# A shorter way from the filters' network to the first unit of a long convolution

## Chip, cores and metric

One core of one Trainium2 chip. The time is the device time of one launch, in microseconds. A measurement is the median of several runs.

## What is computed

The input `x` has 4 images of 64 channels, 256 by 256. Two layers follow each other.

Layer one is a long convolution. Two small networks (X and Y) turn a position embedding `z` (256 x 33) into 64 filters of length 256 each:

```
h = sin(freq * (z @ w1 + b1))
h = sin(freq * (h @ w2 + b2))
h = sin(freq * (h @ w3 + b3))
hx or hy = (h @ wo) * exp(-t * |deltas|)
k[c] = outer(hx[:, c], hy[:, c])
y = x (*) k, causal in both directions, + x * bias[c]
```

Since the kernel of each channel is an outer product, the convolution is one product with a triangular Toeplitz matrix along the rows and one along the columns.

Layer two whitens the channels: the covariance of every ninth sample (64 x 64), its inverse square root by five Newton-Schulz steps, and `out = deconv @ (y - mean)`.

## The kernel before

Everything runs in one program, with an order written out by hand for each engine and semaphores between them. The work has three parts.

**The head.** SP loads `first` (w1 of both networks and z transposed, L202), `columns` (biases and frequency, L203), `hidden` (w2, w3, wo, L208, after POOL has zeroed their place, L337), four x tiles (L216) and the bias (L262). PE makes the first product (L620) once all four parameter loads are in (`params_loaded`, L619). For each of three layers DVE adds the bias and multiplies by the frequency (L465), reduces the argument to the range of the sine table with two steps that find the whole number of turns (L467, L468), three that subtract it times a three-part 2 pi (L470), and a clamp (L471). ACT takes the sine (L417) and PE makes the next product (L624). Between the first layer's argument and the second's, DVE also computes the sampling mask (L474 to L478). At the end DVE scales the decay (L482) and multiplies (L485): `filt` holds 128 filters of 384 values (`filt_ready`).

**The way to the first unit.** SP stores `filt` to DRAM (L265), waits until it has landed, and loads the Hankel tiles of units 0, 1 and 2 (L232, two DMAs per unit, 128 rows of 256 values, each row one value further on, all from this one copy). Then it stores 15 more copies (L271), waits for all of them (`copies_stored`, L273), and only then loads the tiles of units 3 and 4, and in its main loop those of later units, from the 16 copies. For each unit ACT reverses the tile (L391 in fp32, L392 rounded), and DVE makes the remainder of the rounding (L499). For x, ACT rounds (L401) and POOL makes the remainder (L334).

**The units.** There are 128 units (2 sweeps x 64 channels). A unit is V(q) = 16 products in `make_v` and Y(q) = 16 products in `make_y`, both through `toeplitz` (L633 to L636: high by high, high by low, low by high, and one small fp32 product for the other block). PE's order is V(0), V(1), Y(0), V(2), Y(1), V(3), Y(2) and so on. ACT and DVE take V from PSUM (L408, L410, L490), DVE finishes Y (L510), POOL masks it for the covariance (L368) and DVE sums it (L518). SP stores Y to DRAM. Units 0 to 63 and 64 to 127 each cover two images. After them come the covariance (L665), the Newton-Schulz steps (L709 to L728) and the last stage: 64 tiles are read back, multiplied (L744), shifted (L442, L613) and stored to `out` (L287).

SP's queue holds its DMAs in the order written: a wait in it holds back every later DMA. ACT, DVE, POOL and PE go through their lists in order too.

Of the kernel before, what the change touches and what calls it, by code (L numbers as in the profile page):

```python
# [6 lines left out]
F32 = mybir.dt.float32  # L7
# [6 lines left out]
P = 128  # L14
# [15 lines left out]
PI_HI = 6.28125  # L30
PI_MID = math.floor((TWO_PI - PI_HI) * 2.0 ** 21) / 2.0 ** 21
PI_LO = TWO_PI - PI_HI - PI_MID
# [30 lines left out]
def conv_whiten(nc, x, first, hidden, columns, bias, out):  # L63
    g_dram = nc.dram_tensor("filters", [COPIES, COPY_PITCH], F32, kind="Internal").ap()
    y_dram = nc.dram_tensor("convolved", [SWEEPS * P, ROWS * XW], F32, kind="Internal").ap()

    with ExitStack() as ctx:
# [44 lines left out]
        col = sb("col", [P, 4])  # L112
# [3 lines left out]
        arg, turns, hid, pos_f, pos, decay = (kept[:, k * S:(k + 1) * S] for k in range(6))  # L116
# [25 lines left out]
        params_loaded, bias_loaded, w_zeroed = sem("params_loaded"), sem("bias_loaded"), sem("w_zeroed")  # L142
# [5 lines left out]
        copies_stored = sem("copies_stored")  # L148
        x_loaded = [sem(f"x_loaded{k}") for k in range(X_SLOTS)]
# [51 lines left out]
        def _(sp):  # L201
            sp.dma_start(first_sb, first).then_inc(params_loaded, 16)  # L202
            sp.dma_start(col[:], columns).then_inc(params_loaded, 16)  # L203

            sp.wait_ge(w_zeroed, 1)
            for k in range(2):
                h = slice(k * ORDER, (k + 1) * ORDER)
                sp.dma_start(w_sb[h, :, h], hidden[h, :].rearrange("p (l n) -> p l n", l=3)  # L208
                             ).then_inc(params_loaded, 16)
# [8 lines left out]
            def load_hankel(q):  # L218
# [6 lines left out]
                for f in range(2):  # L225
                    at = (f * C + q % C) * GLEN
                    if q < H_SLOTS:
                        src = bass.AP(tensor=g_dram.tensor, offset=at, ap=[[1, P], [1, S]])
                    else:
                        src = bass.AP(tensor=g_dram.tensor, offset=at,  # L230
                                      ap=[[COPY_PITCH + P // COPIES, COPIES], [1, P // COPIES], [1, S]])
# [87 lines left out]
        def _(pool):  # L319
# [16 lines left out]

            nc.gpsimd.memset(w_sb, 0.0).then_inc(w_zeroed, 1)  # L337
# [45 lines left out]
        def _(act):  # L383
            def flip(q):
# [3 lines left out]
                act.wait_ge(hankel_loaded[h], 32 * (q // H_SLOTS + 1))  # L388
# [57 lines left out]
        def _(dve):  # L446
# [14 lines left out]
            dve.wait_ge(params_loaded, 16 * 4)  # L461
            for layer in range(3):

                dve.wait_ge(f_mm, layer + 1)
                chained(nc.vector.tensor_scalar(arg, ps[:, 0, 0:S], col[:, layer:layer + 1], col[:, 3:4],  # L465
                                                ALU.add, ALU.mult))
                chained(nc.vector.tensor_scalar(turns, arg, 1.0 / TWO_PI, MAGIC, ALU.mult, ALU.add))  # L467
                chained(nc.vector.tensor_scalar(turns, turns, MAGIC, None, ALU.subtract))  # L468
                for part in (PI_HI, PI_MID, PI_LO):
                    chained(nc.vector.scalar_tensor_tensor(arg, turns, -part, arg, ALU.mult, ALU.add))  # L470
                nc.vector.tensor_scalar(arg, arg, PI_BELOW, -PI_BELOW, ALU.min, ALU.max).then_inc(f_dve, 1)  # L471
                if layer == 0:
                    dve.wait_ge(index_ready, 1)
                    chained(nc.vector.tensor_copy(idx, index.bitcast(I32)))  # L474
# [303 lines left out]
```

## Time and profile before

| | us |
|---|---|
| median of 3 runs | 952.86 |
| lowest and highest of them | 945.55, 954.18 |
| the profiled execution, its own time | 948.63 |
| its span in the profile | 946.5 |
| V(0) begins on PE | 29.67 |
| last product of the last unit | 641 |

The time of the profiled execution is 2.1 us more than its span; these lie around what the profile records. Products in fp32 are recorded as two instructions each. The profile gives the granted TensorE clock as a share of 2.4 GHz. Its record of the clock here begins at about 34.5 us; ahead of that the column says 1.00 in every slice, also where products take twice as long as later, so that in the head the level has to be read from the length of the products.

### The profile page before, as it was taken

To read this page: it belongs to the slowest core of one execution; us is meant where nothing else is said; L and a number is where in the kernel's file an instruction comes from. 1 tells how busy PE (TensorE), PEld (TensorE's weight loads), DVE (VectorE), ACT (ScalarE), POOL (GpSimd) and SP (SyncE) were. 2 spreads that over 40 slices of the span, in tenths; PEclk is the share of its full clock that TensorE was granted. 3 is DMA by queue.
4 is the path that set the end of the run, shared out by engine and by line. 5 is a ranking of instruction groups with operands and counts; after the bars stand their busy time and mean duration, and the time that the engine had idled before them with its cause. 6 is when DMAs were issued, how large, how long until landed. Compare 5 with 4: busy or idle time off the path is not lost.

```text
span 946.5 us, 15709 instructions
## 1 busy us (share of the span) xinstructions
PE 868.5 (92%) x5970; PEld 729.9 (77%) x5970; DVE 576.3 (61%) x641; ACT 401.0 (42%) x715; POOL 494.5 (52%) x278
## 2 busy tenths in 40 slices
PE   2799999999999999999999999999999997777774
PEld 0799999999999999999999999999544442322221
DVE  5388787788888847878777878784333332222222
ACT  2355555555555525555555555550233322222221
POOL 2298888888888856878777778771000000000000
PEclk9999999999999999999999999999999999999998
DMA  2799998999999866999999999988499999999998
GB/s 105 218 315 293 284 283 276 297 278 291 279 287 287 283 218 194 341 335 339 329 343 332 357 334 330 340 279 331 170 413 422 421 423 427 427 427 427 427 428 360
DMA packets 99351, 306.36 MB, mean 324 GB/s; under 512 B 13484, under 2 KB 48333, under 8 KB 84685
## 3 DMA queue, kind: packets, MB, share of 16 engines
q1 hardware_dynamic: 99276, 305.37, 90.8%
q8 instruction: 47, 0.77, 0.3%
q14 instruction: 28, 0.22, 0.1%
HBM read 167.96 MB, written 137.36 MB: 323 GB/s over the span
## 4 chain that ended last, share of the span: by engine, by line
PE 77%; DMA 18%; DVE 3%; issue 1%; ACT 0%; SPq 0%; DVEq 0%; ACTq 0%
PE ps L636 24%; DMA out<-z_all 17%; PE ps L633 13%; PE ps L634 13%; PE ps L635 13%; PE ps L744 10%; PE ps L665 3%; DVE z_all L613 1%; DVE kept L470 1%; PE ps L684 0%; DMA plain<-filters 0%; PE ps L624 0%; ACT z_all L442 0%; DMA kept<-hidden 0%; PE ps L721 0%
## 5 line engine op out<-in xcount | busy, mean ns | idle before, releaser
L633 PE MATMUL ps<-rounded 128*128 128x256 f32 x1024 | 373.7, 365 | 10.3 <-DVE rounded L499 8.7
L368 POOL TENSOR_TENSOR masked_all<-y_all,mask 128x1024 f32<-128x1024 f32 x126 | 326.3, 2590 | 63.3 <-DVE y_all L510 63.1
L635 PE MATMUL ps<-rounded 128*128 128x256 f32 x1024 | 289.5, 283 | 0.0
L634 PE MATMUL ps<-rounded 128*128 128x256 f32 x1024 | 288.4, 282 | 0.0
L510 DVE SCALAR_TENSOR_TENSOR y_all<-x_all,bias_sb,ps 128x1024 f32<-128x1024 f32 x127 | 162.5, 1280 | 96.8 <-DMA convolved<-y_all 60.5
L334 POOL TENSOR_TENSOR rounded<-x_all,rounded 128x512 fp32r<-128x512 f32 x128 | 165.1, 1290 | 83.1 <-ACT rounded L401 82.5
L633 PEld LDWEIGHTS ps<-rounded 128*128 128x128 f32 x1024 | 196.5, 192 | 11.8 <-issue 11.4
L636 PE MATMUL ps<-plain,x_all 128*128 128x128 f32 x1024 | 197.4, 274 | 0.0
L634 PEld LDWEIGHTS ps<-rounded 128*128 128x128 f32 x1024 | 197.3, 193 | 0.0
L636 PE MATMUL ps<-plain 128*128 128x128 f32 x1024 | 196.4, 273 | 0.0
L635 PEld LDWEIGHTS ps<-rounded 128*128 128x128 f32 x1024 | 192.9, 188 | 0.0
L744 PE MATMUL ps<-kept,z_all 128*128 128x512 f32 x344 | 152.3, 596 | 22.2 <-ACT z_all L442 17.2
L636 PEld LDWEIGHTS ps<-plain,x_all 128*128 128x128 f32 x1024 | 159.0, 191 | 0.0
L636 PEld LDWEIGHTS ps<-plain 128*128 128x128 f32 x1024 | 158.0, 190 | 0.0
L518 DVE TENSOR_REDUCE z_all<-masked_all 128x116 f32<-128x1044 f32 x126 | 155.5, 1234 | 0.0
L744 PEld LDWEIGHTS ps<-kept,z_all 128*128 128x128 f32 x344 | 63.8, 190 | 109.7 <-issue 109.7
L613 DVE TENSOR_SCALAR z_all<-ps,small 128x1024 f32<-128x1024 f32 x48 | 61.6, 1284 | 140.6 <-PE ps L744 75.4
L408 ACT COPY plain<-ps 128x512 f32<-128x512 f32 x128 | 75.0, 586 | 156.1 <-PE ps L636 155.7
L442 ACT ACTIVATE z_all<-ps,small 128x1024 f32<-128x1024 f32 x48 | 53.4, 1113 | 157.2 <-DMA out<-z_all 102.9
L401 ACT CAST rounded<-x_all 128x512 fp32r<-128x512 f32 x128 | 80.2, 626 | 77.4 <-DMA x_all<-x 77.0
L490 DVE TENSOR_TENSOR rounded<-ps,rounded 128x512 fp32r<-128x512 f32 x128 | 87.9, 686 | 28.1 <-ACT rounded L410 27.9
L499 DVE TENSOR_TENSOR rounded<-plain,rounded 128x512 fp32r<-128x512 f32 x128 | 90.7, 709 | 13.4 <-ACT rounded L392 13.4
(103 smaller groups left out, 479.8 us busy)
## 6 DMA issues: line engine op xcount, KB each, us to landing
x_all<-x SPq DMA_DIRECT2D x128, 512.0 KB, 5.6
convolved<-y_all SPq DMA_DIRECT2D x256, 256.0 KB, 5.3
out<-z_all SPq DMA_DIRECT2D x48, 1024.0 KB, 15.7
plain<-filters SPq DMA_DIRECT2D x256, 128.0 KB, 4.8
kept<-convolved SPq DMA_DIRECT2D x29, 1024.0 KB, 19.9
out<-masked_all SPq DMA_DIRECT2D x16, 1024.0 KB, 15.2
kept<-convolved SPq DMA_DIRECT2D x28, 512.0 KB, 6.3
rounded<-convolved SPq DMA_DIRECT2D x9, 1024.0 KB, 20.2
```

The lines of the kernel that those rows point to most:

```text
L334: nc.gpsimd.tensor_tensor(x_lo[k], row_block(q % X_SLOTS, 0), x_hi[k].bitcast(F32), ALU.subtract).then_inc(x_lo_done, 1)
L368: nc.gpsimd.tensor_tensor(masked_of(k, 0, PER), by_image(y_sb[k]), mask_of(q // C, 0, PER), ALU.mult).then_inc(masked_done, 1)
L401: nc.scalar.copy(x_hi[q % 2], row_block(k, 0)).then_inc(x_hi_done, 1)
L490: nc.vector.tensor_tensor(v_lo[k], ps_v[k][:, :, 0:S], v_hi[k].bitcast(F32), ALU.subtract).then_inc(v_lo_done, 1)
L499: nc.vector.tensor_tensor(t_lo[k], hankel[h][:, :, ::-1], t_hi[k].bitcast(F32), ALU.subtract).then_inc(t_lo_done, 1)
L510: nc.vector.scalar_tensor_tensor(y_sb[k], x_sb[q % X_SLOTS], bias_sb[:, q % C:q % C + 1], ps_y[k].rearrange("p a n -> p (a n)"), ALU.mult, ...
L518: nc.vector.tensor_reduce(z_of(q % C), grouped(q % 2, 0, BLOCKS), AX_X, ALU.add).then_inc(z_done, 1)
L633: mm(wide, hi[:, b, cols], t_hi[k][:, f, :], start=True, stop=False)
L634: mm(wide, hi[:, b, cols], t_lo[k][:, f, :], start=False, stop=False)
L635: mm(wide, lo[:, b, cols], t_hi[k][:, f, :], start=False, stop=False)
L636: last = mm(o[:, b, m * S + P:(m + 1) * S], block1[:, b, cols], t_f32[k][:, f, :], start=False, stop=True)
L744: last = mm(ps[:, bank(t, u) + r, :], dmat, t_in[k][:, w:w + IMG], start=True, stop=True)
```

## The change

Three groups of edits:

- **Sine arguments in turns.** A fifth column of `col` gets the frequency divided by 2 pi (once, after `columns` has landed). Per layer DVE now makes three steps: bias and frequency (out of PSUM), adding a constant that rounds to a whole number, and `(rounded - constant) - arg`. The sine takes this remainder with a scale of -2 x 3.1415925. The scaling of the decay moves ahead of the layers, the mask behind `filt_ready`. ACT's `round_x(0)` and `round_x(1)` move behind the sines of the first and the second layer.
- **Own stores and loads for unit 0.** The two filters of unit 0 are stored first, each in one DMA that writes 16 copies of 384 values to a tensor of their own, and loaded from there. The general store is issued between these stores and loads. Every other load stays as it is, in the same order. ACT, DVE and PE take unit 0 filter by filter: V(0) waits for the first filter alone, Y(0) for the second.
- **Products on zeros in pauses.** PE makes 128 x 128 fp32 products on a zeroed tile (POOL zeroes it first of all): 4 ahead of the first product, 4, 6 and 6 in the pauses of the three layers, 22 after the last. The first product waits for `first` alone, the second for `hidden`.

The diff, cut to its core:

```diff
+        rest = kept[:, 14 * S + MASK_COLS:15 * S + MASK_COLS]
+        idle = y_all[:, 0:P]
...
@@ SP @@
                 for f in range(2):
                     at = (f * C + q % C) * GLEN
+                    spread = [[COPY_PITCH + P // COPIES, COPIES], [1, P // COPIES], [1, S]]
+                    if q == 0:
+                        sp.wait_ge(first_stored, 16 * 2)
+                        src = bass.AP(tensor=first_dram.tensor, offset=f * GLEN, ap=spread)
+                        sp.dma_start(hankel[k][:, f, :], src).then_inc(first_hankel[f], 16)
+                        continue
...
             sp.wait_ge(filt_ready, 1)
+            for f in range(2):
+                sp.dma_start(bass.AP(tensor=first_dram.tensor, offset=f * GLEN,
+                                     ap=[[0, 1], [COPY_PITCH, COPIES], [1, GLEN]]),
+                             filt[f * C:f * C + 1, :].unsqueeze(1).to_broadcast([1, COPIES, GLEN])
+                             ).then_inc(first_stored, 16)
             sp.dma_start(bass.AP(tensor=g_dram.tensor, offset=0, ap=[[GLEN, 2 * C], [1, GLEN]]), filt
                          ).then_inc(filt_stored, 16)
+            load_hankel(0)
             sp.wait_ge(filt_stored, 16)
-            for q in range(H_SLOTS):
+            for q in range(1, H_SLOTS):
                 load_hankel(q)
@@ POOL @@
+            nc.gpsimd.memset(idle, 0.0).then_inc(idle_ready, 1)
             nc.gpsimd.memset(w_sb, 0.0).then_inc(w_zeroed, 1)
@@ ACT @@
-            round_x(0)
             for layer in range(3):
                 act.wait_ge(f_dve, layer + 1)
-                nc.scalar.activation(hid, arg, ACT.Sin).then_inc(f_sin, 1)
-            round_x(1)
-            flip(0)
+                nc.scalar.activation(hid, rest, ACT.Sin, scale=-2.0 * PI_BELOW).then_inc(f_sin, 1)
+                if layer < 2:
+                    round_x(layer)
+            for f in range(2):
+                act.wait_ge(first_hankel[f], 16)
+                nc.scalar.copy(t_hi[0][:, f, :], hankel[0][:, f, ::-1]).then_inc(first_hi, 1)
+                flat = nc.scalar.copy(t_f32[0][:, f, :], hankel[0][:, f, :P - 1:-1])
+                flat.then_inc(flipped if f else first_flat, 1)
@@ DVE @@
-            dve.wait_ge(params_loaded, 16 * 4)
+            dve.wait_ge(columns_loaded, 16)
+            nc.vector.tensor_scalar(col[:, 4:5], col[:, 3:4], 1.0 / TWO_PI, None, ALU.mult).then_inc(turns_ready, 1)
+            dve.wait_ge(decay_ready, 1)
+            nc.vector.tensor_scalar(decay[0:C, :], decay[0:C, :], 1.0 / (2 * S), None, ALU.mult).then_inc(turns_ready, 1)
+            dve.wait_ge(turns_ready, 2)
             for layer in range(3):
                 dve.wait_ge(f_mm, layer + 1)
-                chained(nc.vector.tensor_scalar(arg, ps[:, 0, 0:S], col[:, layer:layer + 1], col[:, 3:4],
+                chained(nc.vector.tensor_scalar(arg, ps[:, 0, 0:S], col[:, layer:layer + 1], col[:, 4:5],
                                                 ALU.add, ALU.mult))
-                chained(nc.vector.tensor_scalar(turns, arg, 1.0 / TWO_PI, MAGIC, ALU.mult, ALU.add))
-                chained(nc.vector.tensor_scalar(turns, turns, MAGIC, None, ALU.subtract))
-                for part in (PI_HI, PI_MID, PI_LO):
-                    chained(nc.vector.scalar_tensor_tensor(arg, turns, -part, arg, ALU.mult, ALU.add))
-                nc.vector.tensor_scalar(arg, arg, PI_BELOW, -PI_BELOW, ALU.min, ALU.max).then_inc(f_dve, 1)
+                chained(nc.vector.tensor_scalar(near_int, arg, MAGIC, None, ALU.add))
+                nc.vector.scalar_tensor_tensor(rest, near_int, MAGIC, arg, ALU.subtract, ALU.subtract
+                                               ).then_inc(f_dve, 1)
...
-            split_t(0)
+            for f in range(2):
+                dve.wait_ge(first_hi, f + 1)
+                split = nc.vector.tensor_tensor(t_lo[0][:, f, :], hankel[0][:, f, ::-1],
+                                                t_hi[0][:, f, :].bitcast(F32), ALU.subtract)
+                split.then_inc(t_lo_done if f else first_lo, 1)
@@ PE @@
+            def warm_up(n):
+                for _ in range(n):
+                    mm(ps[:, 5, 0:P], idle, idle, start=True, stop=True)
+            pe.wait_ge(idle_ready, 1)
+            warm_up(4)
+            pe.wait_ge(first_loaded, 16)
             mm(ps[:, 0, 0:S], first_sb[:, 0:2 * ORDER], first_sb[:, 2 * ORDER:], start=True, stop=True
                ).then_inc(f_mm, 1)
             for layer in range(3):
+                warm_up(4 if layer == 0 else 6)
+                if layer == 0:
+                    pe.wait_ge(hidden_loaded, 16 * 2)
                 pe.wait_ge(f_sin, layer + 1)
                 mm(ps[:, 0, 0:S], w_sb[:, layer, :], hid, start=True, stop=True).then_inc(f_mm, 1)
+            warm_up(22)
             pe.wait_ge(filt_ready, 1)
```

## Rows read from the trace of the kernel before

**Rows 1.** The page: span and busy time of each engine.
```profile
span 946.5 us, 15709 instructions
...
PE 868.5 (92%) x5970; PEld 729.9 (77%) x5970; DVE 576.3 (61%) x641; ACT 401.0 (42%) x715; POOL 494.5 (52%) x278
```

**Rows 2.** Stages: length, busy (instructions) of PE, PEld, DVE, ACT, POOL, clock, DMA share, GB/s.
```profile
29.60:34.50 4.90, 4.83 (x22) 4.86 (x23) 0.69 (x1) 0.63 (x2) 0.00 (x0) 1.00 1.04 375
34.50:60.00 25.50, 24.54 (x210) 24.27 (x210) 16.73 (x19) 14.72 (x30) 16.97 (x9) 1.00 0.82 256
...
100.00:460.00 360.00, 359.55 (x3110) 359.39 (x3109) 276.26 (x300) 188.38 (x375) 291.31 (x151) 1.00 0.90 287
```

**Rows 3.** Timeline of the sine layers: start, length, engine, line, operation, idle before.
```profile
0.73 0.43 SPq L202 DMA_DIRECT2D kept<-first  x1
...
4.63 1.22 PE L620 MATMUL ps<-kept 33*128 33x256 f32 x2 [4.63 <-DMA kept<-hidden]
...
5.97 0.54 DVE L465 TENSOR_SCALAR kept<-ps,col 128x256 f32<-128x256 f32 x1 [3.20 <-PE ps L620]
...
7.20 2.29 DVE L470 SCALAR_TENSOR_TENSOR kept<-kept 128x256 f32<-128x256 f32 x3
...
7.76 1.45 POOL L334 TENSOR_TENSOR rounded<-x_all,rounded 128x512 fp32r<-128x512 f32 x1 [4.84 <-ACT rounded L401]
...
16.39 0.54 DVE L465 TENSOR_SCALAR kept<-ps,col 128x256 f32<-128x256 f32 x1 [1.83 <-PE ps L624]
16.97 0.29 DVE L467 TENSOR_SCALAR kept<-kept 128x256 f32<-128x256 f32 x1
...
17.62 1.34 DVE L470 SCALAR_TENSOR_TENSOR kept<-kept 128x256 f32<-128x256 f32 x3
...
19.33 0.42 ACT L417 ACTIVATE kept<-kept 128x256 f32<-128x256 f32 x1 [4.32 <-DVE kept L471]
...
21.16 0.42 DVE L485 TENSOR_TENSOR kept<-ps,kept 128x256 f32<-128x256 f32 x1 [1.09 <-PE ps L624]
```

**Rows 4.** The chain of waits: the second load of the hidden weights.
```profile
2.36 2.23 DMA kept<-hidden
```

**Rows 5.** Timeline of SP's queue: the DMA issues from the filters' store on.
```profile
21.61 0.33 SPq L265 DMA_DIRECT2D filters<-kept  x1
23.48 2.69 SPq L232 DMA_DIRECT2D plain<-filters  x6
26.21 8.44 SPq L271 DMA_DIRECT2D filters<-kept  x15
38.91 3.39 SPq L232 DMA_DIRECT2D plain<-filters  x4
```

**Rows 6.** Timeline, from the first filters loaded to the first unit.
```profile
27.87 0.40 ACT L391 COPY plain<-plain 128x256 f32<-128x256 f32 x1 [7.62 <-DMA plain<-filters]
...
29.67 0.55 PE L633 MATMUL ps<-rounded 128*128 128x256 f32 x1 [8.65 <-DVE rounded L499]
```

**Rows 7.** Timeline of PE at the fourth unit.
```profile
44.66 0.36 PE L633 MATMUL ps<-rounded 128*128 128x256 f32 x1 [0.96 <-issue]
```

**Rows 8.** Timeline of PE in the small matrix products.
```profile
657.30 0.83 PE L684 MATMUL ps<-ident 128*128 128x128 f32 x6
...
661.12 0.49 PE L713 MATMUL ps<-z_all 128*128 128x128 f32 x2
```

**Rows 9.** Table of stages: the loads from one copy, then the copies.
```profile
24.50:26.50 2.00, 0.00 (x0) 0.00 (x0) 0.00 (x0) 0.00 (x0) 0.00 (x0) 1.00 0.62 95
31.00:35.00 4.00, 4.00 (x22) 4.00 (x21) 0.00 (x0) 0.69 (x2) 0.00 (x0) 1.00 1.07 397
```

**Rows 10.** Table of stages: the last stage, and its end.
```profile
669.00:946.00 277.00, 227.88 (x515) 94.77 (x514) 82.33 (x65) 71.25 (x64) 0.00 (x0) 0.99 0.97 405
936.00:938.00 2.00, 0.34 (x1) 0.00 (x0) 1.28 (x1) 1.11 (x1) 0.00 (x0) 1.00 1.00 422
939.00:940.00 1.00, 0.00 (x0) 0.00 (x0) 0.00 (x0) 0.00 (x0) 0.00 (x0) 0.56 1.03 434
```

More of the change, by code:

```diff
@@ L111, in conv_whiten @@
         small = sb("small", [P, 8])
-        col = sb("col", [P, 4])
+        col = sb("col", [P, 5])
         chan_i, chan, rate = sb("chan_i", [P, 1], I32), sb("chan", [P, 1]), sb("rate", [P, 1])
-        arg, turns, hid, pos_f, pos, decay = (kept[:, k * S:(k + 1) * S] for k in range(6))
+        arg, near_int, hid, pos_f, pos, decay = (kept[:, k * S:(k + 1) * S] for k in range(6))
+        rest = kept[:, 14 * S + MASK_COLS:15 * S + MASK_COLS]
+        idle = y_all[:, 0:P]
         pos_i = pos_f.bitcast(I32)
@@ L140, in conv_whiten @@
         ps_y = [ps[:, 4 + 2 * k:6 + 2 * k, :] for k in range(2)]
-        params_loaded, bias_loaded, w_zeroed = sem("params_loaded"), sem("bias_loaded"), sem("w_zeroed")
+        first_loaded, columns_loaded, hidden_loaded = sem("first_loaded"), sem("columns_loaded"), sem("hidden_loaded")
+        bias_loaded, w_zeroed, idle_ready = sem("bias_loaded"), sem("w_zeroed"), sem("idle_ready")
+        first_stored, first_hankel = sem("first_stored"), [sem(f"first_hankel{f}") for f in range(2)]
+        first_hi, first_flat, first_lo = sem("first_hi"), sem("first_flat"), sem("first_lo")
         pool_step, ident_ready = sem("pool_step"), sem("ident_ready")
@@ L201, in _ @@
         def _(sp):
-            sp.dma_start(first_sb, first).then_inc(params_loaded, 16)
-            sp.dma_start(col[:], columns).then_inc(params_loaded, 16)
+            sp.dma_start(first_sb, first).then_inc(first_loaded, 16)
+            sp.dma_start(col[:, 0:4], columns).then_inc(columns_loaded, 16)
             sp.wait_ge(w_zeroed, 1)
@@ L229, in load_hankel @@
                     else:
-                        src = bass.AP(tensor=g_dram.tensor, offset=at,
-                                      ap=[[COPY_PITCH + P // COPIES, COPIES], [1, P // COPIES], [1, S]])
+                        src = bass.AP(tensor=g_dram.tensor, offset=at, ap=spread)
                     sp.dma_start(hankel[k][:, f, :], src).then_inc(hankel_loaded[k], 16)
@@ L387, in flip @@
                 k, h = q % T_SLOTS, q % H_SLOTS
-                act.wait_ge(hankel_loaded[h], 32 * (q // H_SLOTS + 1))
+                act.wait_ge(hankel_loaded[h], 32 * (q // H_SLOTS + (1 if h else 0)))
                 wait(act, y_mm, q - T_SLOTS + 1)
@@ L485, in _ @@
             nc.vector.tensor_tensor(filt[:, 0:S], ps[:, 0, 0:S], decay, ALU.mult).then_inc(filt_ready, 1)
+            dve.wait_ge(index_ready, 1)
+            chained(nc.vector.tensor_copy(idx, index.bitcast(I32)))
+            chained(nc.vector.tensor_scalar(near, idx, 1.0 / STRIDE, MAGIC, ALU.mult, ALU.add))
+            chained(nc.vector.tensor_scalar(near, near, MAGIC, float(STRIDE), ALU.subtract, ALU.mult))
+            chained(nc.vector.tensor_tensor(idx, idx, near, ALU.subtract))
+            nc.vector.tensor_scalar(mask[:], idx, 0.0, None, ALU.is_equal).then_inc(mask_ready, 1)
             def split_v(q):
@@ L644, in make_v @@
                 pe.wait_ge(x_lo_done, q + 1)
-                pe.wait_ge(t_lo_done, q + 1)
+                if q == 0:
+                    pe.wait_ge(first_flat, 1)
+                    pe.wait_ge(first_lo, 1)
+                else:
+                    pe.wait_ge(t_lo_done, q + 1)
                 wait(pe, v_lo_done, q - 1)
@@ L654, in make_y @@
                 pe.wait_ge(v_lo_done, q + 1)
+                if q == 0:
+                    pe.wait_ge(flipped, 1)
+                    pe.wait_ge(t_lo_done, 1)
                 wait(pe, y_done, q - 1)
```

17 lines of the change are left out of this document (3 added, 14 removed).

## The prediction, made before the changed kernel ran

> **What bounds the kernel now.** I read the page first, then the table of stages, then the timeline of the first 45 us engine by engine, SP's queue last. PE is busy for 868.5 of 946.5 us [rows 1], and from 100 to 460 us for 359.55 of 360 [rows 2]. So in the units PE is the bound and has no slack, and whatever lets it begin them sooner comes off the end, if nothing stops it again. The last stage (L744) follows them in order, so it shifts too.
>
> The head is one chain, of which the reader should see the single links [rows 3]. The first product starts at 4.63, when the second load of `hidden` has landed (2.23 after its issue, [rows 4]), and DVE takes it at 5.97. A quiet layer (the third) costs DVE 16.39 to 19.29: 0.58 for L465, 0.33 each for L467 and L468, 1.38 for the three L470, 0.30 for the clamp, starts to starts. In the first layer L470 took 2.29 instead of 1.34, because its last one ran into POOL's split of x (L334, 7.76 to 9.21). `filt` is ready at 21.16 + 0.42 = 21.58. Call this F.
>
> From F on, SP's queue sets the pace [rows 5]: the store at F + 0.03, six loads from F + 1.90, fifteen copies from F + 4.63 to F + 13.1, and, once all have landed, the loads of units 3 and 4 from F + 17.33. The first tile is there at 27.87, V(0) starts at 29.67 = F + 8.1 [rows 6]. V(0) and what follows run at half rate at first: 22 records in 4.9 us against 210 in 25.5 [rows 2]. The record of the clock begins only at 34.5, so the length of the products says that this was the lower level, 1.2 GHz.
>
> One short line is what matters most here: V(3) starts at 44.66 = F + 23.1, after 0.96 us of idle PE [rows 7]. It needs unit 3's tile, whose load SP issues only after all 15 copies have landed, and it follows that issue by 44.66 - 38.91 = 5.75 us. So the units are already caught once by a chain that hangs on F and not on when V(0) began.
>
> **The change, part by part: F.**
> - First product. It waits for `first` alone, issued at 0.73 [rows 3]; with 2.23 to landing [rows 4] that is 2.96. Four products on zeros ahead of it, at the low level 2 x 0.22 each (at the upper level six records, three products, took 0.83 with their tail, [rows 8]), are 1.8 us; if POOL's zeroing ends by 1.1 (an estimate) they end by 2.9. I take 3.0 (2.7 to 3.5). DVE takes the result 1.34 later, at 4.35; its new tiny step and the moved scaling of the decay hang on the exponential, which I put at 3.5, and end near 4.0: hidden, by 0.3.
> - Layer one: L465 0.58, one step like L467 0.33, one like a single L470 0.44, then 0.04 to the sine, 0.42 of sine (L417), 0.05 to PE: done at 6.2. The table load lies ahead of this, behind the exponential. `hidden` was in at 4.63. The second product starts at 6.2 and is taken at 7.55 at the low level.
> - Layer two: its last step would start at 8.45. It has two SBUF inputs, as L470 has, and round_x(0) still ends at about 7.7, since x lands when it did, so POOL's split runs at 7.76 to 9.21 as before. The step then ends at about 9.5 as its like did in [rows 3], 0.6 late. Sine and product follow at 10.0.
> - Layer three: I take PE at the upper level by now (it has been busy nearly without a break since 1.1; before, it rose after 4.9 us of work, [rows 2]). A product of 128 columns takes 0.49 [rows 8], 256 columns 0.21 more, so 0.70 for 1.22. DVE begins at 10.8, its last step at 11.7. POOL's second split (L334) now follows round_x(1), which ends near 10.6, and runs to about 12.0; the step ends at 12.25, 0.1 to 0.5 late. Sine, product 12.75 to 13.5, L485 0.42: F = 14.05.
>
> F thus moves from 21.58 to 14.05, 7.5 us. Without both collisions and with the upper level from the second product on it is 12.6 (9.0 us); with the low level throughout and 6 products on zeros of 0.44 sticking out of a pause of about 2.0 it is 15.0 (6.6 us). The mask (5 steps, 9.8 to 11.6 in the old timeline) hides behind SP's transfers now. The zero products cost nothing in the pauses: 6 x 0.22 = 1.3 against 2.0.
>
> The GPSIMD Engine Reference of the Trainium skill (section Specifications) says that this engine's SBUF interface is shared with VectorE and contends with DVE instructions that have two SBUF inputs. The 2.29 above agrees. By it the two collisions stand; without it F would be some 0.7 to 1.2 earlier.
>
> **From F to V(1).** Two small stores and the general one are issued in about 1.0 (0.33 each, L265), the small ones have landed by F + 2.3 (the store before took 1.87 from issue to the loads), then unit 0's loads take 0.6 to 0.85 each of SP (4 from the copies took 3.39, [rows 5]), so units 1 and 2 are loaded from F + 3.7 instead of F + 2.8. A load with one filter less behind it to reverse and split puts V(0) at F + 6.1 to F + 6.6, against 8.1. If the 22 products on zeros (4.8 us at the upper level, up to 7.3 if it rises on the way) kept the clock, V(0) takes 2.3 instead of 4.3. But V(1) needs unit 1's whole tile: 3.7 + 4.4 (first load to first tile, 23.48 to 27.87) + 1.8 (tile to PE, [rows 6]) = F + 9.8. PE then idles about 1.3. V(1), Y(0), V(2), Y(1) are 64 products, 9.3 us at the upper level, so PE is done at F + 19.1.
>
> **From F to V(3).** Nothing in this part of the chain was shortened. Copies are issued from F + 5.4 instead of F + 4.6. Against that, four loads come from the one copy for six. These run at 95 GB/s where the copies reach 397 [rows 9], so they drag on everything behind them. The two fewer would give 2.4 us if nothing else counted, the later issue takes 0.8. I bound the net at -0.8 to +1.6 and take +0.5: the end of the copies is set by the 397 GB/s, and most of the drag was ahead of it. V(3) is at F + 22.6 = 36.65, against 44.66: 8.0 earlier. PE idles 3.5 us before it, where it was 0.96.
>
> **The clock after this wait.** At 0.96 of idle the upper level held. At the end of the kernel the granted clock is 0.56 in 939 to 940 [rows 10], so it fell at about 939.1, 2.8 us after the last product (0.34 busy after 936). 3.5 us of idle is nearer to this than to 0.96, so I take it that PE falls to the lower level ahead of V(3) and pays again what the head paid: 4.9 us at half rate, 2.4 us. Bounds: 0 and 3.4.
>
> The page TensorE: Matmul & The Clock Gate of the Trainium skill (section on HAM oscillation) tells of a kernel in which DMA waits between short bursts of products brought each burst back to the lower level. By it the fall comes; the last rows of this trace speak for it.
>
> **Sum.** 7.5 (F) + 0.5 (copies) - 2.4 (clock) = 5.6 us. The profiled execution goes from 948.63 to 943.0. The median of the runs shown is 952.86, 4.2 above it, and I forecast for the median: 947.3. The lead at V(0), 29.67 to 20.4, is 9.3 us, and most of what the own stores and loads and the warm clock give over F's gain is thrown away at V(3).
>
> **Rivals.**
> 1. The copies' wait doesn't bind (they land by F + 13). Then what counts is V(1): 33.93 (V(0) of 16 products at 1.07 per four from 29.67) against 14.05 + 9.8 = 23.85, plus 0.3 of slow V(1) and the old 0.96: 11.3 us, 941.5. For it: fewer hot loads. Against it: issue alone needs 8.4 us from F + 5.4, which makes 13.8 even with no landing.
> 2. The clock holds at V(3). 8.0 us, 944.9. For it: 3.5 is a guess by half a microsecond each way, and slow early units would shorten the idle. Against: the 2.8 above.
> 3. Slower than before: the new DRAM tensor lies between `filters` and `convolved` and shifts the latter, which the last stage reads while it writes `out`, 277 us from 669 on at a DMA share near 1 [rows 10]. If the new place lowers this rate by 2% it costs 5.6 us and the gain is gone; from there on it is slower: 4% gives 958. For it: runs of one kernel lie 8.6 us apart, so something in DMA or placement moves it by 0.9%. Against: sizes and strides of `convolved` stay.
> 4. The change does not do what it says: products on zeros don't raise the clock, or they queue in front of the real ones. F = 15.0, PE late everywhere, V(3) after a shorter idle: 6.6 + 0.5 = 7.1 if the clock then holds, 4.7 if not; 946 to 948. It can't be told from the forecast by time, only in the profile.
>
> **How the numbers follow.** Forecast 0.50, rival 1 0.13, rival 2 0.24, rival 3 0.07, rival 4 0.06. A change within 1% (9.5 us) is about what a measurement of this kernel can't tell from none. Forecast, rival 2 and rival 4 lie inside it, rival 1 beyond. Since F alone is open by 1.5 and the measurement by some 3 us, I give a tenth of the forecast and a quarter of rival 2 to faster by over 1%: 0.13 + 0.05 + 0.06 = 0.24. Slower by over 1% needs a rate 5.5% down in rival 3: 0.03. The range runs from 938.5 (rival 1 and a good measurement) to 953.0 (forecast with low F, and the mild half of rival 3).
>
> **What would show it.** Right: F near 14.0, with a DVE step of 0.8 to 1.1 for 0.44 in layers two and three beside POOL's L334; products of 0.70 from the third on; V(0) near 20.4, V(1) near 23.9; a wait of 3 to 4 us before V(3) near 36.6, and 22 records in the next 4 to 5 us. Wrong: V(3) without such a wait (rival 1), products at full rate behind it (rival 2), a last stage longer than 277 us (rival 3), slow products at F (rival 4). The forecast fails outright if F is above 16, or the copies land before F + 14.

## The result, and the profile after

| | us |
|---|---|
| changed kernel, median of 20 runs | 946.17 (942.85 to 952.54) |
| kernel before, median of 20 runs beside them | 952.53 |
| ratio | 0.9948, interval 0.993 to 0.9965 |
| profiled execution, its own time and span | 945.89, 944.1 |

The ratio is taken over the fast executions alone (one of the kernel before, at 1009.42 us, is left out) and is not the quotient of the two medians, which is 0.9933, or 6.4 us. By the ratio the change gains 0.52%, about 5.0 us; 5.6 were forecast, and a median of 947.3. It was measured twice more beside the experiments: 0.9931 (0.9905 to 0.9957) and 0.9947 (0.9918 to 0.9975). The total came out, but not each of its terms: the part from F to V(3) was forecast 2.2 us too short.

The page of the changed kernel: span and busy time.

```profile
span 944.1 us, 15874 instructions
...
PE 880.8 (93%) x6054; PEld 742.9 (79%) x6054; DVE 573.5 (61%) x631; ACT 402.0 (43%) x717; POOL 494.1 (52%) x279
```

PE has 84 records more, the 42 products on zeros. Its busy time therefore grows while the kernel gets shorter; a busy share says nothing about the end here.

The layers in the timeline of the changed kernel (start, length, engine, line and operation, in brackets idle before and what ended it; they answer to [rows 3]):

```profile
3.00 1.22 PE L654 MATMUL ps<-kept 33*128 33x256 f32 x2
...
7.68 1.27 POOL L350 TENSOR_TENSOR rounded<-x_all,rounded 128x512 fp32r<-128x512 f32 x1 [4.61 <-ACT rounded L419]
8.14 1.19 DVE L495 TENSOR_SCALAR kept<-kept 128x256 f32<-128x256 f32 x1
...
9.37 0.55 DVE L496 SCALAR_TENSOR_TENSOR kept<-kept 128x256 f32<-128x256 f32 x1
...
11.90 0.55 DVE L495 TENSOR_SCALAR kept<-kept 128x256 f32<-128x256 f32 x1
...
13.41 0.70 PE L661 MATMUL ps<-kept 128*128 128x256 f32 x2 [0.86 <-ACT kept L434]
...
14.25 0.42 DVE L501 TENSOR_TENSOR kept<-ps,kept 128x256 f32<-128x256 f32 x1 [1.34 <-PE ps L661]
```

The first product starts at 3.00 (forecast 3.0). The collision in layer two is there, but one step earlier than forecast: beside POOL's split of x (L350, 7.68) it is L495, with a single SBUF input, that takes 1.19 us for 0.29. The next step starts only at 9.37. In layer three the same line takes 0.55 beside the second split. The last product takes 0.70 as forecast. F is 14.25 + 0.42 = 14.67, against 21.58 before and 14.05 forecast: 6.9 us for 7.5.

SP's queue from F on (it answers to [rows 5]):

```profile
14.70 1.19 SPq L276 DMA_DIRECT2D first_filters<-kept  x2
15.94 0.58 SPq L280 DMA_DIRECT2D filters<-kept  x1
17.98 1.21 SPq L235 DMA_DIRECT2D plain<-first_filters  x2
19.23 2.01 SPq L241 DMA_DIRECT2D plain<-filters  x4
21.28 8.97 SPq L287 DMA_DIRECT2D filters<-kept  x15
34.47 2.45 SPq L241 DMA_DIRECT2D plain<-filters  x4
```

The two small stores take 0.6 each to issue, where one general store took 0.33; the general store behind them now takes 0.58, so it is not their shape alone. They have landed 3.3 after F, not 2.3. Unit 1's load is issued at F + 4.6 for a forecast 3.7, the copies at F + 6.6 for 5.4. The last copy has landed at 34.47, F + 19.8. Before it was F + 17.3.

PE's waits (they answer to [rows 6, 7]):

```profile
21.43 0.36 PE L672 MATMUL ps<-rounded 128*128 128x256 f32 x1 [2.41 <-DVE rounded L545]
...
26.00 0.36 PE L672 MATMUL ps<-rounded 128*128 128x256 f32 x1 [2.02 <-DVE rounded L522]
...
39.50 0.55 PE L672 MATMUL ps<-rounded 128*128 128x256 f32 x1 [4.05 <-issue]
```

V(0) leads the old one by 8.24 us (29.67 to 21.43), V(1) waits 2.0, and V(3) waits 4.05 and leads by 5.16 only (44.66 to 39.50). Then the clock (stages: length, busy time of PE, PEld, DVE, ACT, POOL, granted clock, DMA share, GB/s):

```profile
25.00:31.00 6.00, 5.00 (x43) 5.04 (x44) 3.25 (x5) 4.03 (x9) 2.04 (x2) 1.00 1.04 381
32.00:34.50 2.50, 2.50 (x24) 2.50 (x24) 0.16 (x1) 0.00 (x0) 2.26 (x1) 1.00 0.11 41
37.00:38.00 1.00, 0.00 (x0) 0.00 (x0) 0.00 (x0) 0.25 (x1) 0.00 (x0) 0.97 0.68 200
38.00:44.00 6.00, 4.50 (x21) 4.53 (x22) 3.12 (x4) 3.09 (x7) 1.33 (x2) 0.50 0.93 269
44.50:45.00 0.50, 0.50 (x5) 0.50 (x4) 0.50 (x1) 0.50 (x2) 0.50 (x1) 0.72 0.96 361
```

The copies fill the DMA to 31 or so (381 GB/s). From 32 to 34.5 nearly nothing moves, yet the last landing comes at 34.47. The granted clock falls to the lower level just ahead of 38 (0.97 in that slice, 0.50 to 44) and comes back at 44.8. PE had been idle since 35.46, so it fell 2.5 us into the idle stretch, and the products from 39.5 to 44.8 ran at half rate: 5.3 us, of which 2.6 are lost (forecast 4.9 and 2.4).

The start of the first covariance (the products of 129 columns behind the first sweep's units) is a mark that lies ahead of the second sweep. Before, and after:

```profile
341.85 3.40 PE L665 MATMUL ps<-z_all 128*128 128x129 f32 x29
```
```profile
338.94 6.31 PE L711 MATMUL ps<-z_all 128*128 128x129 f32 x55
```

2.91 us of lead are left: 5.16 at V(3) less the 2.64 of clock is 2.5 and accounts for all but 0.4 of them. The two profiled spans differ by 2.4 us. The medians differ by more: the old kernel's profiled execution (948.63) lay 3.9 us under its median, and the new one (945.89) 0.3 under its own.

### The profile page after: what moved, and what is told of

The parts are those of the page before. It is cut to its first block, busy times and chain, and to the rows that moved or that the text cites. A ratio compares the mean times of both kernels' runs of the same rounds, so it can differ in the third digit from the quotient of the medians.

```text
span 944.1 us, 15874 instructions
## 1 busy us (share of the span) xinstructions
PE 880.8 (93%) x6054; PEld 742.9 (79%) x6054; DVE 573.5 (61%) x631; ACT 402.0 (43%) x717; POOL 494.1 (52%) x279
## 4 chain that ended last, share of the span: by engine, by line
PE 66%; DMA 24%; DVE 4%; SPq 3%; issue 1%; ACT 0%; DVEq 0%; POOL 0%; ACTq 0%; POOLq 0%
PE ps L675 20%; DMA out<-z_all 17%; PE ps L672 11%; PE ps L673 11%; PE ps L674 11%; PE ps L790 10%; DMA convolved<-y_all 6%; PE ps L711 3%; DVE y_all L533 1%; DVE z_all L640 1%; SPq L251 1%; SPq L241 1%; SPq L220 1%; DMA plain<-filters 0%; PE ps L730 0%
## 5 line engine op out<-in xcount | busy, mean ns | idle before, releaser
L350 POOL TENSOR_TENSOR rounded<-x_all,rounded 128x512 fp32r<-128x512 f32 x128 | 164.9, 1288 | 73.7 <-ACT rounded L419 72.5
```

The lines of the kernel that those rows point to most:

```text
L350: nc.gpsimd.tensor_tensor(x_lo[k], row_block(q % X_SLOTS, 0), x_hi[k].bitcast(F32), ALU.subtract).then_inc(x_lo_done, 1)
```

## The experiments

Theory G is the prediction's: V(3) hangs on the copies and so on F, and lead won behind F is lost there. Theory L says that the lead at V(0) and the warm clock count in full. Every kernel was timed beside the kernel before on the same chip, but on three chips in all, so that kernels of different groups are compared by their ratios. Each ratio has an interval of about 0.25% to either side, some 2.5 us.

**Only the sine arguments in turns.** The changed kernel without the two other groups.

```diff
-            load_hankel(0)
             sp.wait_ge(filt_stored, 16)
-            for q in range(1, H_SLOTS):
+            for q in range(H_SLOTS):
...
-            warm_up(22)
             pe.wait_ge(filt_ready, 1)
```

> Only the sine arguments in turns (with the mask, the decay and the two roundings of x moved), no own loads, no products on zeros; the first product waits for all parameters as before. Theory G (V(3) waits for the 15 copies, which hang on F, the time at which the filters are ready; the lead of V(0) is lost there): F near 16.1, V(0) at F + 8.1 at the lower clock, V(3) at F + 23.1 = 39.2 after about 1 us of idle PE, so the clock holds. That is 5.4 us less than the kernel before, ratio 0.9943, and about 2.5 us less than the changed kernel in the profile, though V(0) starts some 3 us later than there. Theory L (each us of lead at V(0) and the warm clock there count in full): it is slower than the changed kernel by 2.8 us at V(0) and 2 us of clock, together near 5.

Measured: 946.98 us, 0.9958 (0.9932 to 0.9984). PE's two waits in the profile, F being 16.04:

```profile
24.18 0.55 PE L647 MATMUL ps<-rounded 128*128 128x256 f32 x1 [8.70 <-DVE rounded L506]
...
38.88 0.36 PE L647 MATMUL ps<-rounded 128*128 128x256 f32 x1 [0.92 <-issue]
```

V(0) is 2.75 us later than in the changed kernel, and at the lower clock; V(3) is 0.62 us earlier (0.3 ahead of G's 39.2), after 0.92 of idle and with no fall of the clock. The first covariance starts at 334.21, 4.73 ahead of the changed kernel's 338.94: 0.62 of V(3), 2.64 of clock, and the rest from the spacing of the products, which the last section shows. So the head is G's. G's ratio of 0.9943 lies inside the interval, but its order of the two kernels is not seen: this one should have come out 2.5 us below the changed one, and by the ratios it is 1 to 3 us above, which the intervals can't tell from level. What happened to the lead stands further down. L's 5 us above are not there either.

**Only the own stores and loads.** The kernel before with that group.

```diff
+            for f in range(2):
+                sp.dma_start(bass.AP(tensor=first_dram.tensor, offset=f * GLEN,
...
+                             ).then_inc(first_stored, 16)
...
+            load_hankel(0)
```

> Only the own stores and loads of unit 0. Theory G: F stays at 21.6, V(0) starts 1 to 1.5 us earlier, but the copies are issued 2 us later, as in the changed kernel (last landing at F + 19.8 for F + 17.3), so V(3) comes 1.7 us later than in the kernel before, at 46.4, after about 4 us of idle; the clock falls and costs another 2.6. Slower than before by 4.3 us, ratio 1.0045. Theory L: faster by the 1.4 us of lead, ratio 0.9985.

Measured: 952.89 us, 1.002 (0.9993 to 1.0047). The same two starts on PE's timeline:

```profile
28.34 0.55 PE L656 MATMUL ps<-rounded 128*128 128x256 f32 x1 [7.36 <-DVE rounded L541]
...
44.73 0.36 PE L656 MATMUL ps<-rounded 128*128 128x256 f32 x1 [1.82 <-issue]
```

V(0) leads by 1.33 us, V(3) starts at 44.73 for 44.66. The whole lead is gone at the gate. F is 21.54, and SP's queue shows how:

```profile
28.12 8.07 SPq L286 DMA_DIRECT2D filters<-kept  x15
39.61 2.45 SPq L241 DMA_DIRECT2D plain<-filters  x4
```

The copies are issued from F + 6.6, 2.0 us later than in the kernel before, as G has it, but they have landed by F + 18.1 for F + 17.3, and the four loads behind them are issued in 2.45 us for 3.39. G put V(3) 1.7 us too late, and with 1.82 us of idle the clock did not fall. Of the ratios G's 1.0045 lies inside the interval, near its end, and L's 0.9985 just outside; what speaks for the gate is V(3).

**Only the products on zeros** (and the split waits for the parameters).

```diff
-            pe.wait_ge(params_loaded, 16 * 4)
+            pe.wait_ge(idle_ready, 1)
+            warm_up(4)
+            pe.wait_ge(first_loaded, 16)
```

> Only the products on zeros and the split waits of the parameter loads. Theory G: F near 19.2 (first product at 3.0 for 4.6, the last two at the upper clock), V(0) at the upper clock at 27.3, V(3) at F + 23.1 = 42.3 after 3 to 3.5 us of idle, the clock falls there: 2.4 gained and 2.5 lost, ratio 1.000. Theory L: 2.4 of lead and 2.1 of clock count, ratio 0.9953.

Measured: 949.39 us, 0.9967 (0.9943 to 0.9991). F 19.48, V(0) 27.62, V(3) 41.24 after 1.79 of idle, no fall. The copies had landed at F + 16.7 this time. G was wrong here on the fall and by a microsecond on V(3), and its 1.000 lies outside the interval; with V(3) 3.4 us earlier 0.9967 is what G gives without the fall (3.4 of 951.6 is 0.36%). L's 0.9953 lies inside it, so this time doesn't decide between them.

The three groups alone give -0.42, -0.33 and +0.2%: together -0.55%, all at once -0.52%. With intervals of a quarter of a per cent this does not show that they add up. At V(3) they don't: the turns alone lead by 5.8 us, the zeros alone by 3.4, the own stores by -0.1, and all at once by 5.2. The gain comes with the first two groups; none is seen from the own stores and loads.

**The clock held ahead of V(3).** Products on the identity fill the wait.

```diff
                 pe.wait_ge(x_lo_done, q + 1)
+                if q == 3:
+                    pe.wait_ge(v_lo_done, q - 1)
+                    for _ in range(16):
+                        mm(ps[:, 2, 0:P], ident[:], ident[:], start=True, stop=True)
```

> The changed kernel with 16 products on the identity (3.5 us at the upper clock) on PE between Y(1) and V(3), in the pause before the wait. Theory G: V(3) starts at 39.5 as in the changed kernel, but at full rate; 2.6 us less than the changed kernel, ratio to the kernel before near 0.992. Theory L: the pause is of no weight, ratio as the changed kernel's, 0.9948.

Measured: 951.91 us, 0.9987 (0.9959 to 1.0015). The head does what G says: V(3) at 39.0 at full rate, first covariance 2.89 ahead of the changed kernel, in its timeline:

```profile
336.05 9.21 PE L715 MATMUL ps<-z_all 128*128 128x129 f32 x81
```

And yet its ratio is 0.9987 for 0.9948, some 4 us slower. It was measured again, beside the changed kernel:

> The kernel that holds the clock ahead of V(3), once more. Its first trace had V(3) at 39.0 at full rate and the first covariance at 336.05, 2.9 us ahead of the changed kernel's, yet its median lay near that of the kernel before. Theory G: the trace again shows these 2.5 to 3 us at the first covariance, and the lost time lies behind it (stalls of PE on DMA in the second sweep, the last stage), by chance: ratio near 0.992. Rival S: the loss is systematic, the median again 4 to 5 us above the changed kernel's.

> The changed kernel once more, beside the next three on one chip. Both theories: ratio 0.9948, F near 14.7, V(3) near 39.5 after about 4 us of idle, at the lower clock. It also gives a second execution of it to look into: in the traces so far four products took 0.580 or 0.5767 us over long stretches, and the second sweep's stalls differed, so the time at which the covariance of the first sweep begins (338.94 before) may shift by up to 1.8 us from the spacing alone.

Measured: 950.39 us, 0.9973 (0.9948 to 0.9997), against 944.62 us, 0.9931, of the changed kernel, on one chip. So the loss repeats. Again V(3) is early, at 38.4, and at full rate. Both traces show a part of it at the end of the units. The changed kernel there, then the one that holds the clock (DVE's last halves of y, PE's products that keep it busy, and its first product of the second covariance):

```profile
637.38 0.75 DVE L564 SCALAR_TENSOR_TENSOR y_all<-x_all,bias_sb,ps 128x512 f32<-128x512 f32 x1
...
638.07 2.17 PE L730 MATMUL ps<-ident 128*128 128x128 f32 x18
...
641.58 3.59 PE L711 MATMUL ps<-z_all 128*128 128x129 f32 x30 [1.12 <-DVE z_all L575]
```
```profile
639.95 2.17 PE L734 MATMUL ps<-ident 128*128 128x128 f32 x18
...
641.09 0.75 DVE L564 SCALAR_TENSOR_TENSOR y_all<-x_all,bias_sb,ps 128x512 f32<-128x512 f32 x1 [1.88 <-DMA convolved<-y_all]
...
645.20 5.01 PE L715 MATMUL ps<-z_all 128*128 128x129 f32 x28 [2.85 <-DVE z_all L575]
```

DVE waits 1.88 us for a store of y, PE's pause grows from 1.12 to 2.85 us, the clock falls (from 645.7 to 649.1), and the last stage's products (L744 in the kernel before) start 31.9 us after the units' end instead of 28.5 (31.6 in the second trace). In the same microseconds as those stores lies a load of PE's own instructions. The row of that queue in 638 to 639 us, and in 634 to 635 us of the kernel that follows below:

```profile
q8 instruction: 1, 0.02, 5.9%
```
```profile
q8 instruction: 1, 0.02, 11.7%
```

In all three traces of the changed kernel the nearest such loads are 11 to 13 us ahead of the units' end and 7 to 9 us behind it. If their places go by the number of instructions PE has run, 16 more products (64 instructions with their weight loads) moved them. The next pair of kernels tests that.

**The same number of instructions more, elsewhere, and the clock held with no more of them.**

The first kernel is the changed one with

```diff
-            warm_up(22)
+            warm_up(38)
```

and the second the one that holds the clock, with

```diff
-            warm_up(22)
+            warm_up(8)
...
-                    for _ in range(16):
+                    for _ in range(14):
```

> The changed kernel with 38 products on zeros after the last layer instead of 22. They end near 22.5 and put V(0) off by 1.1 us, before a wait of 2 us at V(1) that takes this up; V(3) stays at 39.5. Theory A (alignment): 16 products more shift every load of PE's own instructions by a fixed amount of work; in both traces of the kernel that held the clock one such load fell 2 to 3 us ahead of the units' end, onto the last stores of y, the covariance began 1.5 us later and at the lower clock. The same count here brings the same: from the units' end to L744 31.5 to 32 us for 28.5, median 3 to 4 us above the changed kernel's. Rival N (the place of these loads is of no weight): 28.5, and the changed kernel's median.

> The clock held ahead of V(3) with 14 products, taken out of the 22 after the last layer, so that PE's count of instructions is the changed kernel's. Theories G and A: V(0) and V(1) may run at the lower clock, which the wait for the copies absorbs, V(3) at full rate at 39 to 39.7, first covariance 2 to 3 us ahead of the changed kernel's at equal spacing, units' end to L744 28.5, and now the gain comes through: 2 to 3 us below the changed kernel, ratio near 0.991. Rival S (holding the clock loses in itself): again 4 to 5 us above the changed kernel.

> The changed kernel a third time, on the chip of the other three, as their measure: ratio 0.993 to 0.995, units' end to L744 28.5 us, V(3) near 39.4.

| kernel | median us | ratio | V(3) | first covariance | units' end to L744 |
|---|---|---|---|---|---|
| changed, third time | 945.03 | 0.9947 (0.9918 to 0.9975) | 38.0, low clock | 336.63 | 28.53 |
| 16 products more behind F | 946.82 | 0.9963 (0.9933 to 0.9992) | 38.7 | 334.05 | 30.17 |
| clock held, same count | 944.75 | 0.9943 (0.992 to 0.9967) | 38.4, full | 333.74 | 28.59 |

The end of the first of them, for the rows above:

```profile
637.48 2.17 PE L730 MATMUL ps<-ident 128*128 128x128 f32 x18
...
638.52 0.75 DVE L564 SCALAR_TENSOR_TENSOR y_all<-x_all,bias_sb,ps 128x512 f32<-128x512 f32 x1 [1.80 <-DMA convolved<-y_all]
...
642.66 3.59 PE L711 MATMUL ps<-z_all 128*128 128x129 f32 x30 [2.78 <-DVE z_all L575]
```

Sixteen products in another place bring the wait for the store (1.80), the longer pause (2.78) and the load of instructions 2.5 to 3.5 us ahead of the end; the same number of instructions takes all three away. In the traces of all the other kernels here, where such a load is 4 us or more ahead of the end or behind it, this stretch takes 28.5 to 28.8 us. So the part at the end of the units goes with the number of instructions: 1.4 to 1.7 us of wait, and 1.6 more where the clock falls in it. That the load itself holds up the store is inferred from the times; no run takes it away alone. Its effect on the median is smaller than forecast (1.8 us above the changed kernel, inside the intervals), and in this trace the clock did not fall. Rival S is out: holding the clock does not lose in itself. But G's 2 to 3 us do not arrive either: the medians are 944.75 and 945.03. And of the 2.9 us between the first covariances (333.74 and 336.63) the kept clock, less a V(3) that is 0.4 us later, makes only 1.1; 1.8 come from another spacing of the products, which the last section shows and which falls to an execution by chance as far as is known.

**The gate opened.** Units 3 and 4 come from the one copy too, and the fifth x tile is loaded ahead of the wait for the copies, in the changed kernel and in the kernel before.

```diff
-                    if q < H_SLOTS:
+                    if q < H_SLOTS + 2:
...
+                if k in (5, 10):
+                    load_hankel(H_SLOTS + (k == 10))
+            load_x(4)
             sp.wait_ge(copies_stored, 16 * (COPIES - 1))
-            for q in range(H_SLOTS, 5):
-                load_hankel(q)
```

> The changed kernel with units 3 and 4 loaded from the one copy, issued between the copies (after the 5th and the 10th), and the fifth x tile loaded ahead of the wait for the copies. Theory G: V(3) follows Y(1) near 35.5 with no wait and at full rate, 4.0 + 2.6 = 6.6 us off the changed kernel; first covariance near 332, ratio near 0.988. Rival W: the next transfer behind the copies (unit 5's tile, or the x tiles) becomes the wait, before V(4) or V(5), and gives 3 to 4 us back, ratio 0.992. Theory L: nothing.

> The same edit in the kernel before. Theory G: only its 0.96 us of idle before V(3) goes, ratio 0.999: the gate costs little there because PE starts late. Theory L as well: 0.999 to 1.

Measured: 946.18 us, 0.9925 (0.9896 to 0.9955), and 952.29 us, 1.0004 (0.9981 to 1.0026). The wait of V(3) is gone in both. In the kernel before that was worth nothing, as expected. In the changed one the first covariance starts at 334.65, 4.3 ahead of the first trace of the changed kernel and 2.0 to 2.5 ahead of the two others, not 6.6: the clock was down from 26.3 to 29.7, in V(1), and a new wait stands ahead of V(5), where rival W put it, but small (the profile names no releaser):

```profile
46.80 0.36 PE L674 MATMUL ps<-rounded 128*128 128x256 f32 x1 [0.60 <-issue]
```

Against the changed kernel on the same chip (944.62 us, 0.9931) the total is level. G's 0.988 lies outside the interval, W's 0.992 inside it.

**The gate opened, without the own stores and loads.**

> Turns and products on zeros, no own stores and loads, and units 3 and 4 loaded from the one copy between the copies. Theory G: F near 14.6, V(0) at F + 8.1 = 22.7, V(1) behind it without a wait, V(3) near 34.5 to 36; the own stores bring nothing that this does not, since V(1) to V(2) need the general tiles: ratio as with them (0.9925) or up to 0.002 lower. Theory L: V(0) is 1.3 us later, so 1.3 us slower than with them, 0.994.

Measured: 945.16 us, 0.9941 (0.9911 to 0.997), first covariance at 334.20. V(0) comes 1.6 us later than with the own stores, and its first product takes 0.55 us where it took 0.36, so it runs at the lower clock:

```profile
22.93 0.55 PE L655 MATMUL ps<-rounded 128*128 128x256 f32 x1 [3.73 <-DVE rounded L509]
```

The first covariance is 0.45 us earlier (334.20 for 334.65), but this execution had the faster of the two spacings and the one with own stores the slower; with the 1.8 us of that taken off it is 1.3 us later. So with the gate open the own stores may be worth about as much as their lead at V(0), as L had it. The ratios (0.9941 for 0.9925, both intervals some 0.3% to either side) can't show it. No version beats the changed kernel by more than the intervals.

**Where the lead goes.** The gains of F show at the first covariance in every trace of a kernel that has them, and then run out in part in two stretches. The first is the second sweep, from the first covariance to the units' end: it takes 298.9 us in the first trace of the kernel before and 296.7 to 299.1 in the three of the changed kernel; it takes 302.8 with the turns alone, 303.9 and 300.5 with the clock held, 301.6 with the same count, 303.4 with 16 products more, 300.0 and 301.8 with the gate open, 302.4 with the own stores alone and 300.8 with the zeros alone. With the turns alone PE stalls six times there, 4.2 us together; in the changed kernel once for 0.98 us, and not at all in its other two traces. The longest:

```profile
488.25 0.36 PE L647 MATMUL ps<-rounded 128*128 128x256 f32 x1 [1.39 <-issue]
```

The profile names no releaser for these stalls. The DMA is full around them (share 0.98 to 1.01 from 455 to 555 us in these kernels). From 350 to 640 us DVE waits for stores of y for 42 to 46 us in the three traces of the changed kernel, 55 in the kernel before and 56 to 62 in the turns alone, the zeros alone, the first of the clock held, the same count and the 16 products more. That the loads of PE's instructions decide which of these waits fall due is possible after the experiment above and not shown: the clock held with the same count has 301.6.

The second stretch is the last stage, from its first product to the end of the span: 277.2 us in the kernel before, 277.5, 280.0 and 277.6 in the changed one, 281.2 with the turns alone, 280.5 and 280.7 with the clock held, 276.7 with the same count. With the turns alone the lead of 4.73 over the first trace of the changed kernel is lost by 3.7 us in the second sweep and 3.7 in the last stage; with the clock held the last stage loses 3.0, about as much as the units' end. Why these stretches differ stays open, with one trace per run.

## Why the prediction was right

The time came out inside the range and near the forecast. The mechanism (F sets V(3), the clock falls there) is what the traces show; the size of the sum is in part luck, as the item on the sum says.

- **What bounds the kernel.** Right for the head. V(3)'s wait for the copies is the gate: own stores alone brought V(0) 1.33 us forward and V(3) not at all; the turns alone brought F forward by 5.5 us and V(3) by 5.8, and with units 3 and 4 loaded from the one copy the wait is gone. Only half right behind it: PE has no slack in the first sweep, but in the second it stalls for 0 to 4.4 us by the kernel, so a lead does not come off the end whole.
- **F.** Forecast 14.05, measured 14.67, 14.52 and 14.21 in three traces. The step that was off is the collision in layer two: I put it on the step with two SBUF inputs, from the GPSIMD Engine Reference's rule (section Specifications). The same sentence of the Trainium skill also names instructions in a 2-port mode, and a step with one input is what the trace shows held up: L495 took 1.19 for 0.29 (1.03 and 0.86 in the other two traces). The trace does not name the mode. It starts 0.3 us before the step I had blocked, and the whole layer ends 0.4 later.
- **From F to V(1).** Forecast F + 9.8, measured F + 11.3. The stores' issue (0.6 for 0.33) and landing (3.3 for 2.3 after F) were mis-sized. It cost nothing, since V(1) had slack to the gate. Nor did the 22 products on zeros keep the clock for V(0) each time: they did in the first trace, and in the other two V(0) ran at half rate, which the wait of V(1) took up.
- **The copies.** This is the term that failed: "+0.5", bounded at -0.8 and +1.6. Measured in the first trace: V(3) at F + 24.8 for 23.1, -1.7, outside the bounds; F + 24.7 and F + 23.8 in the others. SP reached the copies 2.0 us later behind F, not 0.8: 1.4 of that is the wait until the own stores have landed (F + 3.3, where the general store had by F + 1.9), the rest the loads, of which unit 0's take 0.6 each where all took 0.45. The two fewer loads from one copy did not give this back: in the eight traces with own stores and the wait of V(3) the last copy had landed at F + 18.1 to F + 19.8, in the three without own stores at F + 16.7 to F + 17.3. How much is lost differs by execution: the own stores alone stand at the low end and lost nothing at V(3). What sets it was not found.
- **The clock at V(3).** Right, and rival 2 is out for the changed kernel: it fell in all three traces. The price was 2.6 us in the first (forecast 2.4), 2.8 in the second and 1.7 in the third, where it was back by 41.5. The kernels with 0.9 to 1.8 us of idle there did not see it fall.
- **The sum.** For the profiled pair the terms measured are 6.9 - 1.7 - 2.6 = 2.6, and both the first covariance (2.9) and the spans (2.4) show this. The second trace gives 2.7 and, its faster spacing taken off, 2.9 at the first covariance; the third gives 4.9 and 5.2. So the 5.6 forecast matches the ratio's 5.0 better than its own terms do, and that is luck: the term of the copies was too good by 2.2 us in the first trace, and what made up for it in the median was not in the sum. The old kernel's profiled execution was a fast one, and the second sweep and the last stage, which I took as unmoved, differ between kernels and executions by up to 7 and 4.5 us.
- **Rivals.** 1 (the copies' wait doesn't bind) is out: 4.05, 3.94 and 3.00 us of idle. 3 (a slower last stage by placement): 277.5, 280.0 and 277.6 us in the changed kernel, 277.2 before; the kernel before with another order of loads had 278.3 and the turns alone, without the new tensor, 281.2, the longest of all. The new tensor is not what moves it. 4 is out: the clock had risen by the third product (0.79 us), and the fourth took 0.70.

## What to carry to other kernels

A lead won at the start is worth what is left of it at the next wait that doesn't depend on it: look for the short idle stretch behind the place that you speed up (0.96 us here), and work out from what it hangs. A small transfer put ahead of others on one queue delays them by its issue and by any wait for it (2.0 us here at the copies), even if what it loads arrives sooner. Where a difference of half a per cent is to be explained, compare marks in the middle of the trace as well as the end: here leads of 3 to 8 us were plain at the first covariance while the total swung by as much in the stages behind it. And compare them at the same spacing of the products: 1.8 us of difference at that mark were no work of any edit.

## What the runs showed of the hardware that was not expected

**Loads of instructions count.** PE's own instructions come by DMA, 25 loads from 100 to 460 us in the kernel before, one in about 14 us. Where one fell into the last stores of y, DVE got its buffer 1.5 to 1.9 us later; with 16 products more ahead it fell there, with the old number it did not. The Trainium skill (Runtime: NRT & Kernel Launch, Instruction fetch mechanics) gives one load per 256 instructions and calls its cost mostly hidden. The first agrees with the trace: in those 360 us 6219 products and weight loads are recorded, 249 to a load. The second is about the instructions themselves; what the traces suggest here is a price for another transfer.

**Two spacings of the same products.** Over long stretches four products take 0.580 us in some executions and 0.5767 in others, both at the upper clock. The first products of 25 groups in 200 to 214 us, kernel before and turns alone:

```profile
199.66 0.36 PE L633 MATMUL ps<-rounded 128*128 128x256 f32 x1
...
213.58 0.36 PE L633 MATMUL ps<-rounded 128*128 128x256 f32 x1
```
```profile
199.76 0.36 PE L647 MATMUL ps<-rounded 128*128 128x256 f32 x1
...
213.60 0.36 PE L647 MATMUL ps<-rounded 128*128 128x256 f32 x1
```

13.92 / 24 = 0.580 and 13.84 / 24 = 0.5767. The changed kernel had the first in two executions and the second in one, so it is not the program alone. Of the other traces the first sweep has 0.580 with the zeros alone, both times with the clock held, and with the gate open in the kernel before and in the changed one, and 0.5767 with the own stores alone, the same count, the 16 products more and the gate open without own stores. Over the first sweep it makes 1.8 us: from V(3) to the first covariance 297.2 in the kernel before, 295.3 with the turns alone. In every trace the second sweep begins at 0.5767. What sets it was not found.

**The clock can fall soon.** Ahead of V(3) in the changed kernel it went down 2.5 us after PE stopped, and with 16 products more behind F it stayed up through 2.9 us of idle at the same place. Ahead of V(0) PE idles 2.4 to 2.5 us in all three traces of the changed kernel. In the first V(0) ran at the upper level (first product 0.36 us); in the others the clock fell 2.0 and 2.5 us after PE stopped. The second, with PE's line and the row of its clock (0.50):

```profile
21.30 0.55 PE L672 MATMUL ps<-rounded 128*128 128x256 f32 x1 [2.44 <-DVE rounded L545]
```
```profile
21.00:24.00 3.00, 2.70 (x12) 2.73 (x13) 0.58 (x2) 0.60 (x2) 0.00 (x0) 0.50 0.89 156
```

The length of the pause alone does not settle it.
